# Attention scores from rounded parts: queries and keys split in two, three products for one

## The reference, cut to what matters

```
x  = x @ conditioned_weight[b] + bias
q, k, v = x @ wq[h], x @ wk[h], x @ wv[h]
q, k = rope(q), rope(k)            # the first half of the features is rotated, the second kept
p  = softmax(causal(q @ k.T / 128))
x  = x + concat_h(p @ v) @ wo
```

## Time and profile before

| what | before |
|---|---|
| median of 3 runs | 926.9 us |
| the profiled execution, its own time | 926.78 us |
| its span in the trace | 925.5 us |
| granted TensorE clock | 1.00 |
| TensorE busy | 911.2 us (98%) |
| VectorE busy | 528.7 us (57%) |
| ScalarE busy | 444.4 us (48%) |
| GpSimd busy | 269.8 us (29%) |

### The profile page before, as it was taken

One profiled execution on the slowest core, in us unless ns is written; L12 is line 12 of the kernel. 1 busy time (PEld: TensorE's weight loads), 2 busy tenths in 40 slices (PEclk: granted clock), 3 DMA queues, 4 the chain that ended last, 5 costly groups with the idle time before them and its releaser, 6 DMA issues.

```text
span 925.5 us, 13114 instructions
## 1 busy us (share of the span) xinstructions
PE 911.2 (98%) x4859; PEld 767.9 (83%) x4859; DVE 528.7 (57%) x975; ACT 444.4 (48%) x827; POOL 269.8 (29%) x242
## 2 busy tenths in 40 slices
PE   8999999999999999999999999999999999999998
PEld 4768868887799999998888888888888888888886
DVE  6754454578757766785665564333333335688544
ACT  3665566434355455572343343343343442345775
POOL 1533321310475765653400152041140230010000
PEclk9999999999999999999999999999999999999999
DMA  8030001220445343432503013003003011000011
GB/s 301 30 114 23 24 1 69 104 81 28 121 129 157 125 126 126 126 125 77 180 18 148 12 24 137 0 1 137 1 8 129 1 55 83 1 0 1 1 46 46
DMA packets 22192, 67.47 MB, mean 73 GB/s; under 512 B 4514, under 2 KB 11954, under 8 KB 19314
## 3 DMA queue, kind: packets, MB, share of 16 engines
q1 hardware_dynamic: 16546, 40.15, 11.9%
q0 software_dynamic: 5440, 26.50, 9.9%
q10 hardware_dynamic: 144, 0.00, 0.0%
HBM read 55.09 MB, written 9.45 MB: 70 GB/s over the span
## 4 chain that ended last, share of the span: by engine, by line
PE 89%; DVE 4%; issue 2%; DMA 2%; ACT 2%; POOL 1%; SPq 0%; ACTq 0%; DVEq 0%; POOLq 0%
PE banks L1112 18%; PE banks L1114 18%; PE banks L1113 18%; PE banks L1365 5%; PE banks L1367 5%; PE banks L1366 5%; PE banks L1206 3%; PE banks L1190 3%; PE banks L1404 2%; PE banks L1403 2%; PE banks L1197 2%; PE banks L1417 1%; PE banks L1416 1%; PE banks L1160 1%; DMA weight_stage<-in_cond_w 1%
## 5 line engine op out<-in xcount | busy, mean ns | idle before, releaser
L1112 PE MATMUL banks<-input_hi,mlp_hi 128*128 128x512 f32 x376 | 147.6, 392 | 0.0
L1114 PE MATMUL banks<-input_hi,mlp_lo 128*128 128x512 f32 x376 | 146.4, 389 | 0.0
L1113 PE MATMUL banks<-input_lo,mlp_hi 128*128 128x512 f32 x376 | 146.4, 389 | 0.0
L1631 ACT CAST hidden_hi<-hidden 128x512 fp32r<-128x512 f32 x96 | 59.6, 621 | 158.6 <-DVE hidden L2048 107.5
L2237 POOL TENSOR_TENSOR mlp_lo<-weight_stage,mlp_hi 128x768 fp32r<-128x768 f32 x32 | 59.1, 1846 | 172.4 <-ACT mlp_hi L1609 172.4
L2054 DVE TENSOR_TENSOR hidden_lo<-hidden,hidden_hi 128x512 fp32r<-128x512 f32 x96 | 66.4, 692 | 61.7 <-ACT hidden_hi L1631 61.4
L2048 DVE SCALAR_TENSOR_TENSOR hidden<-banks,L_expert_weight,gelu 128x512 f32<-128x512 f32 x64 | 48.0, 750 | 83.6 <-PE banks L1114 80.5
L1625 ACT ACTIVATE gelu<-banks 128x512 f32<-128x512 f32 x96 | 57.4, 598 | 71.2 <-PE banks L1114 63.5
L1114 PEld LDWEIGHTS banks<-input_hi,mlp_lo 128*128 128x128 f32 x376 | 70.6, 188 | 14.8
L1113 PEld LDWEIGHTS banks<-input_lo,mlp_hi 128*128 128x128 f32 x376 | 70.6, 188 | 14.4
L1112 PEld LDWEIGHTS banks<-input_hi,mlp_hi 128*128 128x128 f32 x376 | 70.6, 188 | 14.2
(11 more groups left out here) (350 smaller groups left out, 2148.8 us busy)
## 6 DMA issues: line engine op xcount, KB each, us to landing
weight_stage<-in_packF SPq DMA_DIRECT2D x8, 1536.0 KB, 7.0
weight_stage<-in_shared SPq DMA_DIRECT2D x2, 3072.0 KB, 11.2
expert_output<-y_rows SPq DMA_DIRECT2D x40, 128.0 KB, 1.8
weight_stage<-in_cond_w SPq DMA_DIRECT2D x4, 512.0 KB, 5.3
residual<-in_xT SPq DMA_DIRECT2D x4, 512.0 KB, 10.7
first_half_swapped<-first_half SPq DMA_DIRECT2D x16, 128.0 KB, 2.0
routed_input<-x_rows SPq DMA_DIRECT2D x16, 128.0 KB, 1.7
weight_stage<-in_ffn_w SPq DMA_DIRECT2D x2, 1024.0 KB, 7.1
```

The lines of the kernel that those rows point to most:

```text
L1112: pe.matmul(o, wh, dh, start=(i == 0), stop=False)
L1113: pe.matmul(o, wh, dl, start=False, stop=False)
L1114: last = pe.matmul(o, wl, dh, start=False, stop=(i == len(terms) - 1))
L1631: act.copy(hiD[n % 4][:, :], prod_t[n % 2][:, :]).then_inc(done)
```

## The change

Queries and keys are no longer kept as fp32 tiles but as a rounded part (`queries_hi`, `keys_hi`) and the rest (`queries_lo`, `keys_lo`). A score product becomes three: hi with hi, hi with the rest of the keys, rest of the queries with hi. A diagonal piece of 128 columns is computed 256 wide. The new steps of a rotation:

- *rope_1* on VectorE now adds cosines and sines for all 128 partitions, in place of one half, into `times_cos`.
- *turn_hi* on ScalarE rounds the sum into the hi tile, in two casts of 64 partitions.
- *rope_lo* on VectorE and *rope_0* on GpSimd subtract the hi tile from the sum, 64 partitions each.
- *skip* writes the kept half into the hi tile, and *skip_lo* on VectorE forms the rest from PSUM, bias and hi tile, in two instructions of 64 partitions. A kept product's bank is now free after skip_lo, no longer after skip.

Keys and values lie in three slots of one chunk each, queries in two. One conditioned weight, its mask, the bias row and the staged output weights share their place with `down_by_row`, so the loads of `ld_pack0` wait for three more units. In the order: in chunk 0 the values come behind the new steps; the first product of the rotation of k in chunk 1 stands ahead of all scores; the rotation of q and k of chunk 2 comes before the split of input 3.

Two places of the order, on the engines that the new steps share with the softmax.

The diff, cut:

```diff
@@ first_rotated
-        run(value_tiles(0))
+            act.append(("turn_hi", "k" if w == "q" else "q", 0))
+            pool.append(("rope_0", "k" if w == "q" else "q", 0))
         for w in ("k", "q"):
             dve.append(("sines", w, 0))
-            pool.append(("rope_0", w, 0))
-        for w in ("k", "q"):
             dve.append(("rope_1", w, 0))
+        dve.append(("skip_lo", "q", 0))
+        dve.append(("rope_lo", "k", 0))
+        dve.append(("skip_lo", "k", 0))
+        dve.append(("rope_lo", "q", 0))
+        run(value_tiles(0))
@@ rotated
         dve.append(("cosines", w, c))
+        dve.append(("skip_lo", w, c))
         yield
         if c == 1:
             yield
         dve.append(("sines", w, c))
         dve.append(("rope_1", w, c))
+        act.append(("turn_hi", w, c))
         pool.append(("rope_0", w, c))
         yield
+        dve.append(("rope_lo", w, c))
@@ plan
+    coming = rotated("k", 1)
+    next(coming)
-    run(weave(weave(attention(0), chain(rotated("k", 1), rotated("q", 1), value_tiles(1))), ...
+    run(weave(weave(attention(0), chain(coming, rotated("q", 1), value_tiles(1))), ...
-    run(weave(attention(1), chain(some(fold, 2), later_input(2), fold, later_input(3), rotated("k", 2), rotated("q", 2), value_tiles(2))))
+    run(weave(attention(1), chain(some(fold, 2), later_input(2), fold, rotated("k", 2), rotated("q", 2), value_tiles(2), later_input(3))))
@@ FREED
-"kept": "skip"
+"kept": "skip_lo"
@@ tensor_program, S
-                for n0 in range(0, width, CH):
-                    n1 = min(n0 + CH, width)
-                    pe.matmul(o[:, n0:n1], qT[c % 2][:, h, qs], kT[c // CPB][:, h, n0:n1], start=True, stop=(n1 < width))
+                spans = [(c - 1, 0, CH)] if c % CPB else []
+                spans.append((c, width - (i + 1) * P, max((i + 1) * P, PAIR)))
+                q_hi, q_lo = qH[c % 2][:, h, qs], qL[c % 2][:, h, qs]
+                for of, n0, n in spans:
+                    pe.matmul(o[:, n0:n0 + n], q_hi, kH[of % SLOTS][:, h, 0:n], start=True, stop=False)
+                    if of == spans[0][0]:
+                        for w in ("k", "q"):
+                            pe.wait_ge(*ready("rope_0", w, c))
+                            pe.wait_ge(*ready("rope_lo", w, c))
+                            pe.wait_ge(*ready("skip_lo", w, c))
+                    pe.matmul(o[:, n0:n0 + n], q_hi, kL[of % SLOTS][:, h, 0:n], start=False, stop=False)
+                    pe.matmul(o[:, n0:n0 + n], q_lo, kH[of % SLOTS][:, h, 0:n], start=False, stop=(of != c))
@@ scalar_program
+            elif kind == "turn_hi":
...
+                act.wait_ge(*ready("rope_1", w, c))
+                dst, _ = turned_halves(w, c)
+                act.copy(dst[0:P // 2, 0, :], cos_t[n][0:P // 2, :])
+                act.copy(dst[P // 2:P, 1, :], cos_t[n][P // 2:P, :]).then_inc(done)
@@ vector_program
-                dve.tensor_tensor(dst[P // 2:P, 1, :], cos_t[n][P // 2:P, :], sin_t[n][P // 2:P, :], ALU.add).then_inc(done)
+                dve.tensor_tensor(cos_t[n][:, :], cos_t[n][:, :], sin_t[n][:, :], ALU.add).then_inc(done)
+            elif kind == "skip_lo":
...
+                dve.wait_ge(*ready("skip", w, c))
+                dve.scalar_tensor_tensor(lo[0:P // 2, 1, :], o[0:P // 2, :], bs[0:P // 2, :], f(hi[0:P // 2, 1, :]), ALU.add, ALU.subtract)
+                dve.scalar_tensor_tensor(lo[P // 2:P, 0, :], o[P // 2:P, :], bs[P // 2:P, :], f(hi[P // 2:P, 0, :]), ALU.add, ALU.subtract).then_inc(done)
+            elif kind == "rope_lo":
...
+                dve.wait_ge(*ready("turn_hi", w, c))
+                h = 1 if c else 0
+                half = slice(h * P // 2, (h + 1) * P // 2)
+                dve.tensor_tensor(lo[half, h, :], cos_t[n][half, :], f(hi[half, h, :]), ALU.subtract).then_inc(done)
@@ pool_program
-                pool.tensor_tensor(dst[0:P // 2, 0, :], cos_t[n][0:P // 2, :], sin_t[n][0:P // 2, :], ALU.add).then_inc(done)
+                pool.wait_ge(*ready("turn_hi", w, c))
+                h = 0 if c else 1
+                half = slice(h * P // 2, (h + 1) * P // 2)
+                pool.tensor_tensor(lo[half, h, :], cos_t[n][half, :], f(hi[half, h, :]), ALU.subtract).then_inc(done)
@@ pool_program, ld_pack0
+                pool.wait_ge(*ready("bias_in"))
+                pool.wait_ge(*ready("fold", 0, KD - 1, 1))
+                pool.wait_ge(*ready("wo_lo"))
```

More of the change, by code:

```diff
@@ L303, in plan @@
     share_banks(False)
-    run(weave(weave(attention(0), chain(rotated("k", 1), rotated("q", 1), value_tiles(1))), chain([None] * 3, conditioned_half(4, G))))
+    coming = rotated("k", 1)
+    next(coming)
+    run(weave(weave(attention(0), chain(coming, rotated("q", 1), value_tiles(1))), chain([None] * 3, conditioned_half(4, G))))
     dve.append(("half_mask",))
@@ L748 @@
 FREED = {
-    "bias_row": "row_in", "fold_bias": "bias_in", "fold": "fold_lo", "same": "same_in", "kept": "skip", "v": "v_row",
+    "bias_row": "row_in", "fold_bias": "bias_in", "fold": "fold_lo", "same": "same_in", "kept": "skip_lo", "v": "v_row",
     "S": "exp", "T": "p_col", "PV": "o_lo", "out": "resid",
@@ L767 @@
     "hid_lo": "hidden_lo", "he_lo": "hidden_lo", "hm_lo": "hidden_lo", "hf_lo": "hidden_lo", "hot_lo": "hidden_lo", "onehot": "hidden_lo",
-    "down": "out_of_hidden", "w2": "out_of_hidden", "dn": "out_of_hidden", "f2": "out_of_hidden", "hot": "out_of_hidden", "last_hot": "out_of_hidden", "f2_of": "out_of_hidden", "hot_add": "add", "last_gate": "xe", "last_gate_in": "add", "wm_pre": "wm_hi",
+    "down": "out_of_hidden", "w2": "out_of_hidden", "dn": "out_of_hidden", "f2": "out_of_hidden", "hot": "out_of_hidden", "last_hot": "out_of_hidden", "f2_of": "out_of_hidden", "hot_add": "add", "last_gate": "xe", "turn_hi": "skip", "skip_lo": "rope_1", "rope_lo": "rope_1", "last_gate_in": "add", "wm_pre": "wm_hi",
 }
@@ L903, in program @@
     sin_t = [sb("times_sin", [P, CH]) for _ in range(2)]
-    cwF = [sb("cond_weight", [P, KD, D]) for _ in range(B)]
-    cmask = sb("cond_mask", [P, KD, D])
-    brow = sb("bias_row", [1, 2, FH])
+    cwF = [None, sb("cond_weight", [P, KD, D])]
     projected_top = top[0]
-    kT = [sb("keys", [P, NH, T]) for _ in range(B)]
-    qT = [sb("queries", [P, NH, CH]) for _ in range(2)]
-    vR = [sb("values", [P, TPB, D]) for _ in range(1)]
+    kH = [sb("keys_hi", [P, NH, CH], F32R) for _ in range(SLOTS)]
+    kL = [sb("keys_lo", [P, NH, CH], F32R) for _ in range(SLOTS)]
+    qH = [sb("queries_hi", [P, NH, CH], F32R) for _ in range(2)]
+    qL = [sb("queries_lo", [P, NH, CH], F32R) for _ in range(2)]
+    second = sb("values", [P, QT, D])
     scored_top = top[0]
-    vR.append(sb("values", [P, TPB, D]))
+    vR = [sb("values", [P, QT, D]), second, sb("values", [P, QT, D])]
     ptT = [sb("probT", [P, TPB, PAIR]) for _ in range(2)]
-    woS, woH, woL = sb("out_weights", [P, KD, D]), sb("out_weights_hi", [P, KD, D], F32R), sb("out_weights_lo", [P, KD, D], F32R)
+    woH, woL = sb("out_weights_hi", [P, KD, D], F32R), sb("out_weights_lo", [P, KD, D], F32R)
     vbias = sb("value_bias", [P, NH])
@@ L1082, in with_router, with turned_halves @@
         return ap[:, 2 * KD * H0:2 * KD * H0 + HT * DW].rearrange("p (k n) -> p k n", n=DW)
+    def turned_halves(w, c):
+        hi, lo = (qH, qL) if w == "q" else (kH, kL)
+        n = c % len(hi)
+        return hi[n][:, :, :], lo[n][:, :, :]
     def qt_of(c, i):
@@ L1776, in vector_program @@
                     dve.wait_ge(*ready("rope_0", *rope_units[n - 2]))
-                    dve.wait_ge(*ready("rope_1", *rope_units[n - 2]))
+                    dve.wait_ge(*ready("rope_lo", *rope_units[n - 2]))
                 if c % CPB:
```

41 lines of the change are left out of this document (26 added, 15 removed).

## The result

The change takes 947.12 us, the median of 8 runs (945.44 to 951.31), against 927.17 for the kernel before on the same chip: 1.0218 times as long, 95% interval 1.0204 to 1.0232. That is 20 us slower, where 9.3 had been forecast, and above the range.

The account below looks back on a forecast made before the run. TensorE, busy for 98% of the span with no wait over 0.6 us after its start, was taken to bound the kernel. 7.0 + 3.1 + 0.5 - 1.3 = +9.3 on 926.78 gave 936.1 us, range 924 to 941.

Parts of the forecast that it names:

- Score price: TensorE's score products in all chunks: three rounded products of 512 columns take 0.77 us for 0.87, saving 2.3 us in all.
- 0.64 per head: Score tiles of chunks 1 and 3: TensorE time saved per head by the rounded products, 0.64 us.
- Cheaper passes win: Rival on scores: they save 6.4 us as columns say and chunk 0's chains cost half, 924.4 us; chance 0.17.
- Start of chunk 0: First score of chunk 0: its second product waits for rope_lo q until 32.05, a net delay of 1.3 us.
- First transpose: T(0,0,0) in chunk 0: behind skip_lo k1, maximum, reciprocal and norm, at 38.0; 2.9 us more, TensorE idle 3.2.
- Rest of chunk 0: T(0,0,0) to S(1,0,0): waits of 0.7, 1.5, 1.3 and 0.2 us, adding 2.8; S(1,0,0) at 54.8, +7.0 so far.
- Chunk 1: Chunk 1: bank waits at the second output product (+1.7) and kept q2 (+2.7), less 1.3 on scores: +3.1 us.
- waits of chunk 0 only: Rival: chunk 1's two bank waits vanish because TensorE comes late or ScalarE early; +4.9 us, 931.7; chance 0.20.
- Chunk 2: Chunk 2: the second value product waits 0.7 us for its bank behind turn_hi q3; +0.5 us (0 to 1).
- Chunk 3: Chunk 3: it rotates nothing, so the change is -1.3 us (-0.5 to -2).
- the new steps mostly fit: Chunk 2: long P·V products of chunk 1 stand beside the new steps, which mostly fit; +0.5 us in all.
- The clock: Rival: TensorE's clock falls in the wait before T(0,0,0); 937.9 us, or 940 with a second wait; chance 0.12.

Follow-up runs that it names:

- the second profile of the change: The same kernel as the change, nothing altered, run once more beside the follow-up experiments; this profiled run took 944.79 us, the median there 946.24 us.
- e1: Kernel before, with queries and keys rounded and every score formed as three equal rounded products, no rests and no new order: 925.2 us, 0.9986.
- e4: The change, with VectorE's skip_lo for chunks 1 and 3 one step of the weave later: 947.93 us, 1.023.
- e6: The change, with TensorE kept busy in its eight longest waits by products that nobody reads: 943.59 us, 1.0181.
- e9: Kernel before with three equal rounded score products, plus the change's order of units and none of its new steps: 931.89 us, 1.0061.
- e11: Kernel before with one plan line altered: the split of chunk 3's input stands last in chunk 1's side work: 931.8 us, 1.0047.
- e3: The change, with turn_hi and rope_0 one step of the weave later and rope_lo behind them: 945.84 us, 1.0207.
- rounding: The change without skip_lo, rope_lo and rope_0, its two products with a rest made hi with hi again: 936.07 us, 1.0104.
- the five moves: The change with split back, skip_lo later for chunk 1, turn_hi later, three half pieces behind maxima, chunk 3's rope_0 behind a norm: 936.12 us, 1.0096.
- the three tried one at a time: The change with one move each: chunk 3's split back, 944.26 us; turn_hi later, 945.84 us; skip_lo later for chunks 1 and 3, 947.93 us.

## Why the prediction was right or wrong

The direction and the main mechanism were right: waits in front of TensorE outweigh the cheaper scores. The size was half, and for chunk 2 the mechanism was missed. Term by term, forecast against the second profile of the change:

- **Score price.** Pitches as forecast (0.78 for 0.77); in all 1.3 instead of 2.3 saved (e1), in part since waits that were hidden behind the longer products show. (The 0.64 per head is 0.66 by the prediction's own terms, 0.1 us in all.) "Cheaper passes win" is out.
- **Start of chunk 0.** Second product of S(0,0,0) at 32.54, forecast 32.05. Four new steps of VectorE in six instructions, not five steps, stand ahead of the first maximum. The rows on which it rests:

```profile
29.61 0.74 DVE L1835 SCALAR_TENSOR_TENSOR keys_lo<-banks,folded_bias,keys_hi 64x512 fp32r<-64x512 f32 x1
30.37 0.76 DVE L1836 SCALAR_TENSOR_TENSOR keys_lo<-banks,folded_bias,keys_hi 64x512 fp32r<-64x512 f32 x1
31.16 1.13 DVE L1844 TENSOR_TENSOR queries_lo<-times_cos,queries_hi 64x512 fp32r<-64x512 f32 x1
```

  and GpSimd beside it:

```profile
30.47 1.27 POOL L2213 TENSOR_TENSOR queries_lo<-times_cos,queries_hi 64x512 fp32r<-64x512 f32 x1 [1.44 <-issue]
```

  skip_lo, with one input from PSUM, keeps its 0.76 beside a GpSimd addition; rope_lo, with both inputs in SBUF, ends 0.55 after GpSimd does. The Trainium skill (SBUF — State Buffer, section Who interferes with whom) has the rule that a reading GpSimd instruction locks out a VectorE instruction with two SBUF inputs and not one with a single SBUF input; the trace agrees.
- **First transpose.** T(0,0,0) at 38.82 after 3.21 us of idle PE, forecast 38.0 after 3.2; the reason (maximum behind skip_lo) is shown by e4.
- **Rest of chunk 0.** T(0,1,0) 1.39 (forecast 1.5), PV(0,0,3) 1.04 (1.3). T(0,0,2), forecast at 0.7, does not wait here, since PE reaches it late, at the low clock; with the clock up (e6) it waits 1.07. S(1,0,0) is 8.6 late, not 7.0: 0.8 of it the first transpose. Of the other 0.8 about half goes with the low stretch (T(0,0,0) to S(1,0,0) takes 17.66 us here and 17.24 in e6, where the clock stays up); the rest was not traced.
- **Chunk 1**, +5.7 for +3.1. The two bank waits came at the size worked out, 1.92 (2.1) and 2.68 (2.7), so "waits of chunk 0 only" is out too. The reason given for the second, kept q2, is only half of it. It is 1.47 in e9 and 1.23 in e11, which have no turn_hi, and 2.61 in e3, where turn_hi stands behind the exponential. In e11 the exponential ahead of the copy of same q2 waits for a maximum that stands behind x1_lo, sines and rope_1 on VectorE:

```profile
79.33 0.90 ACT L1497 ACTIVATE weight_stage<-banks,softmax_stats 128x768 f32<-128x768 f32 x1 [2.74 <-DVE softmax_stats L1801]
```

  So turn_hi adds some 1.2 to a wait that the order makes; that the sum came out close is partly luck. Not seen were same k2 (1.06) and the second value product of chunk 2 (0.74).
- **Chunk 2**, +4.1 for +0.5. This is **the step that failed**: "the new steps mostly fit". The diff moves the split of chunk 3's input behind the values. The prediction priced what that puts ahead of the output products in chunk 1, but gave the moved split itself no term. It puts x0_lo directly ahead of same k3 (1.85) and same k2 one step nearer to its fold; alone it costs 4.5 us (e11), a part of which lies in the wait of kept q2. The part of the sum on chunk 0 saw a copy stuck behind turn_hi at PV(0,0,3), and the part on chunk 2 did not look for its twin at T(2,0,0) (1.65). The 0.7 that it did forecast there, for the second value product, came out at 0.29.
- **Chunk 3**, -0.7 for -1.3: the mis-sized score gain.
- **The clock**, a rival at 0.12 and 1.8 to 4 us, fell in every run of the change: 0.998 to 0.991. It is worth some 2.7 us between medians (e6). Part of what a low stretch costs is hidden in the wait that follows (T(0,0,2) above). It is not a case of its own: it comes with the waits.

The misses in S(1,0,0), chunks 1, 2 and 3 are 1.6 + 2.6 + 3.6 + 0.6 = 8.4, and 9.3 + 8.4 = 17.7, the lag at the last score tile (141.42 before, 159.13). The second profile, at clock 0.998, took 944.79 us; the median of the eight runs, 947.12, lies 2.3 higher, at lower clocks. By kernels, each median less that of before beside it: products -1.1, order +6.8, rounding +4.0, rests +10.2, in all 19.9. How each share divides between waits and clock was measured for the whole only. Nor do the shares tell work from place: the five moves won back 9.9 us across them.

## What to carry to other kernels

On a kernel whose bound engine never waits, price every line that a diff moves, a split of an input too: name its first reader and what now stands between them. Where an in-order engine gets an operation that waits for another engine, put it behind whatever the bound engine will need meanwhile; five such moves, the split among them, were worth 10 of the 20 us here, and the three tried one at a time showed little of it. And where a change brings several waits of one to three microseconds, price clock falls together with them, not as a separate accident, though not every wait brings one.

## What the runs showed of the hardware that was not expected

The granted clock falls behind waits much shorter than the 3.78 us by which the prediction went. In the first profile of the change it is at 0.50 from 34.6 on, behind waits of 0.54 and 0.97 us, and near 205 us behind a single one, outside the attention:

```profile
204.39 0.39 PE L1130 MATMUL banks<-expert_hi,hidden_hi 128*128 128x264 f32 x1 [1.87 <-DVE x_rows L1894]
```

Not every such wait does it. At the same place the second profile of the change waits 1.62 us and the clock stays at 1.00:

```profile
199.57 0.39 PE L1130 MATMUL banks<-expert_hi,hidden_hi 128*128 128x264 f32 x1 [1.62 <-DVE x_rows L1894]
```

In e9 a wait of 1.94 there is followed by a fall; in e11 waits of 0.76, 1.23 and 1.99 leave the clock at 1.000 in all five runs, and so does one of 1.51 us in the kernel before, near 239 us. Which wait does it differs from run to run (five stretches in one profile of the change, one in the other). This is part of why the times of the change spread over 5.9 us, those of before over 3.2; 1.0 of it is the late start of the first profile. The Trainium skill (TensorE: Matmul & The Clock Gate, section A second HAM failure mode: psum-queue depth-cycling) tells of a clock that swings between its two levels where TensorE often idles briefly between groups of products; the trace agrees that brief idling can do it, here behind single waits and not each time.

And the slow pitch at the start (0.42 us for 512 columns) stands under a granted clock of 1.00 in the profile of before, from 3.7 to 8.8 us. So the reading of the prediction, that this is the 1.2 GHz level, is not borne out by the clock's own column. The low stretches show both a pitch of 0.43 (from 42.47 to 42.90 in the first profile) and 0.50, but that speaks for them only. What slows the first products was not tried.
